# A graph layer on one core: edge tables and reciprocals move from VectorE to ScalarE, and the f32 selection tables read a PSUM ramp

## What is computed

```
xn = layernorm(x)
msg  = xn[src] * edge_weight                    # segment mean per (relation, target), 8 relations
gnn  = einsum(mean of msg, weight) + xn @ root + bias
q, k = elu(xn @ wq + bq) + 1, elu(xn @ wk + bk) + 1 ;  v = xn @ wv + bv       # 8 heads
mix  = ((q @ (k^T v)) / (q . sum(k) + 1e-6)) @ wo + bo
x1 = x + gnn + mix
f  = layernorm(x1)
out = x1 + sum over the 2 best of 6 experts (routing weight * three-layer MLP of f)
```

## Time and profile before

| | |
|---|---|
| time, median of 3 runs | 3027.47 us (3027.4 to 3027.52) |
| the profiled execution | 3028.82 us, its span 3027.3 us |
| PE | 2934.1 us busy (97% of the span) |
| DVE | 2189.2 us (72%) |
| ACT | 1765.7 us (58%) |
| POOL | 1659.3 us (55%) |
| mean granted TensorE clock | 0.988 of full speed |

### The profile page before, as it was taken

One profiled execution on the slowest core, in us unless ns is written; L12 is line 12 of the kernel. 1 busy time (PEld: TensorE's weight loads), 2 busy tenths in 40 slices (PEclk: granted clock), 3 DMA queues, 4 the chain that ended last, 5 costly groups with the idle time before them and its releaser, 6 DMA issues.

```text
span 3027.3 us, 47261 instructions
## 1 busy us (share of the span) xinstructions
PE 2934.1 (97%) x16707; PEld 2567.4 (85%) x16708; DVE 2189.2 (72%) x5317; ACT 1765.7 (58%) x3392; POOL 1659.3 (55%) x1700
## 2 busy tenths in 40 slices
PE   6999999969989999999999999999999999999998
PEld 5888878858778888888888888888888888888887
DVE  4479664125668787778888777788777778878775
ACT  3555555523446665666666566666666566666555
POOL 1000000042257777777777777777777777777740
PEclk9999999989999999999999999999999999999999
DMA  7677677875443444444444444443444444344420
GB/s 258 249 267 272 261 276 269 292 250 174 146 140 107 129 131 132 133 127 129 118 121 133 133 134 129 131 122 118 134 131 131 134 126 129 116 128 131 131 74 11
DMA packets 182224, 473.45 MB, mean 156 GB/s; under 512 B 46934, under 2 KB 105260, under 8 KB 159747
## 3 DMA queue, kind: packets, MB, share of 16 engines
q0 software_dynamic: 80544, 221.54, 25.4%
q1 hardware_dynamic: 99248, 247.02, 22.6%
q10 hardware_dynamic: 2196, 1.86, 0.2%
HBM read 312.80 MB, written 158.29 MB: 156 GB/s over the span
## 4 chain that ended last, share of the span: by engine, by line
PE 68%; DVE 6%; ACT 2%; DVEq 1%; issue 1%; DMA 1%; SPq 0%; ACTq 0%
PE bank L1647 45%; PE acc L1704 8%; PE acc L1710 8%; PE acc L1647 2%; DVE sel L1362 2%; PE bank L1674 1%; PE bank L1810 1%; DVE x L1457 1%; PE bank L1683 1%; PE bank L1693 1%; DVE stats_c L1461 1%; PE bank L1760 1%; DVEq L1459 1%; DVE h_lo L1487 1%; ACT h_hi L1205 1%
## 5 line engine op out<-in xcount | busy, mean ns | idle before, releaser
L1135 POOL DMA_INDIRECT ring<-y_tab,tab x1666 | 1642.6, 986 | 653.4 <-issue 497.5
L1205 ACT ACTIVATE h_hi<-bank,bias_t 128x512 fp32r<-128x512 f32 (+1 forms) x600 | 407.7, 679 | 315.6 <-PE bank L1647 280.1
L1487 DVE TENSOR_TENSOR h_lo<-bank,h_hi 128x512 fp32r<-128x512 f32 (+1 forms) x600 | 382.1, 675 | 228.1 <-ACT bank L1206 226.2
L769 PE MATMUL yb<-wr_hi,xhl 128*128 128x512 f32 x1568 | 509.4, 402 | 14.5 <-ACT yst L350 12.5
L1192 ACT ACTIVATE row_hi<-ring,tab 128x256 fp32r<-128x256 f32 x1091 | 449.6, 497 | 14.4 <-PE acc L1710 13.5
L1379 DVE SCALAR_TENSOR_TENSOR row_lo<-ring,tab,row_hi 128x256 fp32r<-128x256 f32 x1091 | 447.8, 478 | 7.8 <-ACT row_hi L1192 7.8
L350 ACT ACTIVATE yst<-yb 128x512 f32<-128x512 f32 x392 | 229.8, 596 | 273.6 <-PE yb L769 245.5
L1206 ACT ACTIVATE bank<-bank,bias_t 128x512 f32<-128x512 f32 (+1 forms) x600 | 386.3, 644 | 0.0
L769 PEld LDWEIGHTS yb<-wr_hi,xhl 128*128 128x128 f32 x1568 | 298.6, 190 | 88.8 <-ACT yst L350 15.2
L1647 PE MATMUL bank<-ew_hi,h_hi 128*128 128x256 f32 x1176 | 342.7, 291 | 1.5 <-DVE h_lo L1487 1.4
L1647 PE MATMUL bank<-ew_lo,h_hi 128*128 128x256 f32 x1176 | 329.1, 280 | 0.0
(11 more groups left out here) (265 smaller groups left out, 5514.7 us busy)
## 6 DMA issues: line engine op xcount, KB each, us to landing
y_tab<-yst SPq DMA_DIRECT2D x97, 1024.0 KB, 4.1
ring<-y_tab,tab POOLq DMA_INDIRECT x1666, 2.8
xt_tab<-xhl SPq DMA_DIRECT2D x25, 1024.0 KB, 4.6
xk<-xt_tab SPq DMA_DIRECT2D x25, 1024.0 KB, 4.9
xc<-xt_tab SPq DMA_DIRECT2D x25, 1024.0 KB, 5.4
x<-x_tab SPq DMA_DIRECT2D x49, 256.0 KB, 3.2
xs<-in_x SPq DMA_DIRECT2D x24, 512.0 KB, 6.0
x_tab<-xs SPq DMA_DIRECT2D x24, 512.0 KB, 5.0
```

Source lines behind the costliest of these rows:

```text
L769: last = pe.matmul(out_ap, a, b, start=(i == 0), stop=(i == len(parts) - 1))
L1135: pool.indirect_dma_start(out=out_ap, out_offset=None, in_=y_tab[:, :], in_offset=bass.IndirectOffsetOnAxis(ap=idx_ap, axis=0)).then_inc(s ...
L1205: act.activation(dest[:, m, 0:W], b[:, 0:W], ACT.Relu, bias=bias)
L1487: gone(dve.tensor_tensor(lo_[:, m, 0:W], bank[plan[kind, (e, m)][0]][:, 0:W], hi[:, m, 0:W].bitcast(F32), ALU.subtract))
```

## The change

Three edits, all in the second part.

1. `weighted` reads `ramp` (PSUM) in place of `iota_w` (SBUF): every one of the 575 `sel` instructions.
2. `tables` moves to ACT: four activations of 128x17 (identity plus a bias, which is minus the tile's first node, from a new table `neg_t` that POOL writes at the start). In the loop they stand behind `high` of expert 3 in place of the same expert's end on DVE. Tables 0 and 1 are made ahead of all key work on ACT. DVE's `weighted` waits for a new semaphore, `rel_set`.
3. The copy of the reciprocals over features moves to ACT (`by_feature`): one activation of 128x1024, which waits for DVE's reciprocal (`rden_set`). In the loop it stands behind `gate_t` and ahead of `high` of portions 5 and 6.

```diff
+            neg_t = sbuf(pc, "neg_t", [P, TROWS])
...
             @block.gpsimd
+                pool.iota(neg_t[:, :], pattern=[[-NT, TROWS]], base=0, channel_multiplier=0,
+                          allow_small_or_imprecise_dtypes=True).then_inc(neg_set, 1)
...
             @block.scalar
+                def by_feature(i):
+                    act.wait_ge(rden_set, i + 2)
+                    act.activation(rden_c[:, :, :].rearrange("p t (h d) -> p (t h) d", h=HEADS),
+                                   rden[:, :, :].rearrange("p t h -> p (t h)").unsqueeze(2)
+                                   .to_broadcast([P, SUB * HEADS, C // HEADS]), ACT.Copy).then_inc(rden_ready, 1)
+
+                def tables(n):
+                    act.wait_ge(tab_in[n % 2], 16 * SUB * (n // 2 + 1))
+                    for t in range(SUB):
+                        last = act.activation(rel_w[:, n % 2, t, :], tab[:, n % 2, t, :, 1], ACT.Identity,
+                                              bias=neg_t[:, SUB * n + t:SUB * n + t + 1])
+                    last.then_inc(rel_set, 1)
...
                             gone(act.activation(gate_t[:, 0:W], take(i, plan, "gt", 0)[0:GROWS, 0:W], ACT.Copy))
+                        if more and e == 1:
+                            by_feature(i)
                         for p in SPLIT_AT.get(e, ()) if more else ():
                             high(i + 1, p)
+                        if more and e == EXPERTS - 3 and i + 2 < SUPER:
+                            tables(i + 2)
...
+                act.wait_ge(neg_set, 1)
+                tables(0)
+                tables(1)
                 for p in range(PARTS):
...
                     if p == KEYED + 1:
...
+                        by_feature(-1)
...
             @block.vector
                     dve.drain()
-                    dve.reciprocal(rden[:, :, :], rden[:, :, :])
-                    dve.drain()
-                    dve.tensor_copy(rden_c[:, :, :].rearrange("p t (h d) -> p (t h) d", h=HEADS),
-                                    rden[:, :, :].rearrange("p t h -> p (t h)").unsqueeze(2)
-                                    .to_broadcast([P, SUB * HEADS, C // HEADS])).then_inc(rden_ready, 1)
+                    dve.reciprocal(rden[:, :, :], rden[:, :, :]).then_inc(rden_set, 1)
...
-                def tables(n):
-
-                    dve.wait_ge(tab_in[n % 2], 16 * SUB * (n // 2 + 1))
-                    for t in range(SUB):
-                        dve.tensor_scalar(rel_w[:, n % 2, t, :], tab[:, n % 2, t, :, 1], float(n * NS + t * NT), None,
-                                          ALU.subtract)
-                    dve.drain()
-
                 def weighted(n, p):
                     if p >= parts(n):
                         return
+                    dve.wait_ge(rel_set, n + 1)
                     tables_free(dve, n, p)
                     for q, (t, k) in enumerate(tiles_of_portion(p)):
-                        last = dve.tensor_scalar(sel[:, p % BUFS, q, :], iota_w[:, :], rel_w[:, n % 2, t, k:k + 1],
+                        last = dve.tensor_scalar(sel[:, p % BUFS, q, :], ramp[:, 0:NT], rel_w[:, n % 2, t, k:k + 1],
                                                  tab[:, n % 2, t, k, 2:3], ALU.is_equal, ALU.mult)
...
-                        if more and e == EXPERTS - 3:
-                            if i + 2 < SUPER:
-                                tables(i + 2)
```

More of the change, by code:

```diff
@@ L969, in gps_layer @@
             emptied = {"act": sem("act_emptied"), "dve": sem("dve_emptied")}
-            rden_ready, acc_full, x1_done = (sem(n) for n in ("rden_ready", "acc_full", "x1_done"))
+            rden_set, rel_set, rden_ready, acc_full, x1_done = (sem(n) for n in ("rden_set", "rel_set", "rden_ready", "acc_full", "x1_done"))
             var_c, std_c, xn_c, d_ready, ex_ready, gap_ready, g2_ready, gate_ready = (
@@ L987, in gps_layer @@
             rows_in = [sem(f"rows_in{g}") for g in range(SLOTS)]
-            xtab_in, xold_in, xrows_in, xrows_split, xsum_done, xnew_set, xnew_out, base_set, x_tab_done, xsum_free = (
+            xtab_in, xold_in, xrows_in, xrows_split, xsum_done, xnew_set, xnew_out, base_set, neg_set, x_tab_done, xsum_free = (
                 sem(n) for n in ("xtab_in", "xold_in", "xrows_in", "xrows_split", "xsum_done", "xnew_set", "xnew_out",
-                                 "base_set", "x_tab_done", "xsum_free"))
+                                 "base_set", "neg_set", "x_tab_done", "xsum_free"))
             def tiles(plan):
@@ L1573, in _ @@
                 dve.memset(zv[:, :, :, :], 1.0)
-                tables(0)
+                dve.drain()
                 for p in range(PARTS):
@@ L1604, in _ @@
                                           ALU.subtract).then_inc(w_split_c, 1)
-                tables(1)
                 prepare(1, 0)
```

## The result

The changed kernel takes 3063.09 us (median of 4 runs, 3062.6 to 3064.68) against 3027.43 us for the kernel before in the same session: 1.0122 times as long, 95% interval 1.0108 to 1.0137. It is slower by 36 us, and the profiled execution's span grew by 34.5 us, from 3027.3 to 3061.8. Where this time lies can be read from five views of the changed kernel.

The account below looks back on a forecast made before the run. The loop was taken as bound by PE and its turn-end wait for DVE's y; ramp 18.5, copy 15.6 and start 1.5 us sum to 35.6, giving 3063 us, own range 3052 to 3075, 8 in 10 from 3042 to 3086.

Parts of the forecast that it names:

- What bounds the kernel: In the loop PE is the bound; its one recurring wait is for DVE's y at a turn's end, 0.57 us.
- faster: Rival: sel from PSUM begins sooner, shrinking the turn-end wait, worth 13.4 us in all; 3016 without an expert 1 stall; chance 0.06.
- The ramp from PSUM: Twelve sel columns at a turn's end, each 67 ns slower: 0.80 us a turn, +18.5 us (0 to 37).
- The copy over features: ACT's copy in expert 1 delays portion 5's rows 0.97 us against 0.43 slack: 0.65 us x 24, +15.6 us.
- the cold start: In expert 1, PE restarting behind its stall without weights loaded ahead: 0.1 us added, chosen between nothing and 0.39.
- One sign: Expected trace sign in expert 1: DVE's wait for row_hi grows from 0.33 to about 2 us.
- The tables: Four small activations moved to ACT in expert 3, where nobody waits for them: nothing.
- The start: Key features begin 6 us later, covered by PE's 7.76 us wait; portion 11's rows late after key work: +1.5 us.
- The sum: Whole run: 18.5 + 15.6 + 1.5 = 35.6 us more, giving a median of 3063 us.
- one stays away: Rival: the turn-end stall or the expert 1 stall doesn't come, about 3046 us; chance 0.15.
- the two last: Rivals "faster" (3016 without an expert 1 stall; chance 0.06) and no difference, both additions hidden (3027; chance 0.06).
- More than the sum: Rival: turn-end idle of 1.4 us drops PE's clock, up to 3101, or PSUM source at upper bound, 3082; chance 0.13.

Follow-up runs that it names:

- e8: Kernel before with none of the edits, but six sel columns moved behind the additions to y at a turn's end; 3015.56 us, ratio 0.9959.
- e9: Kernel before with tables on ACT and six sel columns moved behind the additions to y at a turn's end; 3019.27 us, ratio 0.9964.
- f2: Kernel before with sel made four ways by portion: PSUM or SBUF source, 64 or 128 columns an instruction; a single execution, 3105.52 us.
- e1: Changed kernel with sel reading the ramp in SBUF again; tables and copy over features stay on ACT; 3044.52 us, ratio 1.0059.
- e3: Kernel before with one edit alone, tables made on ACT; 3026.65 us, ratio 1.0001.
- e2: Changed kernel with the copy over features back on DVE; PSUM ramp and tables on ACT stay; 3046.84 us, ratio 1.0069.
- e4: Kernel before with one edit alone, sel reading the ramp in PSUM; 3047.45 us, ratio 1.0069.
- e5: Changed kernel with ACT's copy over features moved behind the rows of portion 5; 3045.13 us, ratio 1.0047.
- e6: Changed kernel with six of the twelve sel columns at a turn's end moved behind the additions to y; 3029.61 us, ratio 0.9997.
- e7: Changed kernel with the copy moved behind portion 5's rows and six sel columns behind the additions to y; 3022.92 us, ratio 0.9976.
- f1: Changed kernel with ACT's copy over features made three times in a row in expert 1; 3145.49 us, ratio 1.0383.
- f3: Kernel before with tables on ACT, six sel columns behind the additions to y and one extra gather a block; 3038.17 us, ratio 1.0038.

## Why the prediction was right, step by step

- **What bounds the kernel.** Right. Every run in which the wait for `y` at a turn's end grew or shrank moved the time with it. What I hadn't read is the second bound close beneath: POOL waits for PE for only 11.8 us of the loop's 2048, by the same view of waits. My rival "faster" put the turn's end at 13.4 us; with PE's restarts it is 19, of which the loops of e8 and e9 got 7, nearly all of it in their first seven or eight turns; behind these the gathers kept it.
- **The ramp from PSUM.** Forecast 67 ns a column, 0.80 us a turn, 18.5 us. Measured 63 ns (0.319 less 0.256), a run of twelve longer by 0.75 us, PE's wait longer by 1.31 - 0.57 = 0.74 us, 17 us over 23 turns; alone it cost 0.0069, 21 us, with 17 to 25 in the interval. The rate was right and the start unchanged (f2). The Trainium skill ("VectorE: DVE Perf Modes", "Why PSUM operands drop a tier") has the rate so, and f2's 1.05 ns a column agree. The longer start of the Trainium skill's cycle table (the same page, "The TRN2 errata"), which by the prediction's estimate would have made 131 ns a column, isn't in these runs. The five columns ahead of `ft_lo` stayed hidden.
- **The copy over features.** The mechanism was right in each link; the size was a little small. The delay of 0.97 us was 0.94, the slack of 0.43 was 0.40, and `y` came 0.54 us after the moment at which PE would have gone on (its last product's start and one pitch, 1648.76 + 0.23 = 1648.99, against 1649.53). That this is the forecast to the hundredth is luck: two errors of 0.03 us cancel. The term that was mis-sized is the cold start, "a choice" of 0.1 us: PE begins 0.06 us after `y` ends and needs 0.34 us for its first product where the pitch is 0.23, so 0.17 us. 0.71 x 24 = 17 us in place of 15.6; e1 less e3 gives 0.0058, 18 us. The wait that the view of waits shows, 0.43 us, is not the price: it counts from the modelled end of the last product, 0.16 us after the next could have begun. One sign was misread: DVE's wait for `row_hi` was to grow to about 2 us and is 1.29. DVE spends the 0.69 us that it saves on the copy ahead of this place, where it waits for PE's bank before the first additions to `y` (0.89 us in the changed kernel, 0.17 before).
- **The tables.** Next to nothing, as forecast (e3: 1.0001). A turn of e3 takes 87.63 us against 87.58, and one of e2 88.38 against e4's 88.33: 0.05 us, which no ratio here can tell.
- **The start.** The steps happened. ACT's rows and PE's waits in the trace of the changed kernel:

```profile
642.97 0.94 ACT L1197 ACTIVATE rel_w<-tab,neg_t 128x17 f32<-128x17 f32 x4 [8.62 <-DMA tab<-etab]
643.92 1.28 ACT L1271 ACT_TABLE_LOAD   x1
645.22 0.42 ACT L1271 ACTIVATE ek_c<-zv 128x256 f32<-128x256 f32 x1
...
646.45 1.23 PE L1819 MATMUL bank<-zv,kf_c 128*128 128x129 f32 x4 [9.81 <-DVE kf_c L1571]
...
659.15 0.50 PE L1656 MATMUL bank<-wkv_hi,xk 128*128 128x512 f32 x1
...
885.75 0.39 PE L1719 MATMUL acc<-row_hi,hot_r 128*128 128x256 f32 x1 [1.10 <-DVE row_lo L1392]
```

  Key features begin at 645.22 (forecast 645 in place of 638.70), PE waits 9.81 us for them, and yet the third block's products begin at 659.15, where they began at 659.18: the delay went into the cover. At the end of the key work portion 11's rows cost 1.10 us (forecast 1.5). What I had not seen is that the cover has a price of its own, and that it fell. The idle 7.76 us before 659.18 were followed by a low clock; now PE works up to then. The same stretch by windows, before and after:

```profile
659.10:664.00 4.90, 4.82 (x13) 4.00 (x14) 1.02 (x2) 0.72 (x2) 3.68 (x5) 0.50 0.69 239
```
```profile
659.10:664.00 4.90, 4.86 (x26) 4.16 (x26) 2.68 (x6) 2.04 (x6) 3.73 (x4) 1.00 0.85 295
```

  13 products against 26 in the same time. The low clock now stands at the first key products behind the wait of 9.81 us (646.4 to 651.1: 15 products, at 0.50), and its loss fits into the cover too. The move is worth about 2.5 us in a trace: the products of the key work's last portion but one begin at 880.01 in place of 882.75, and behind portion 11 block 0's gates still come 1.2 us earlier (929.84 against 931.01). So the start gained in these two traces what the forecast had it lose. But it is lost in the scatter of the runs: over the traces with the old start (the kernel before, e4, e8, f2) these gates lie between 928.7 and 932.7 us, over those with the whole new one (the changed kernel, e1, e5, e6, e7, f1) between 928.2 and 931.8; and e3, in which the low clock moves too, is not measurably faster.
- **The sum.** 35.6 us forecast, 34.5 in the span. The turns split it more sharply than the ratios do. A turn, from gates to gates, takes 89.10 us in place of 87.58: 1.52 us more, 1.45 forecast. The ramp has 0.75 of it (e4: 88.33), the copy 0.72 (e1 less e3: 88.35 less 87.63), the tables 0.05. So the terms were 17.2 us (forecast 18.5), 17.3 over 24 turns (15.6), 1.2 (nothing) and, for the start, -1.2 (+1.5). Errors of 1.2 to 2.7 us with opposite signs cancelled. That the sum is closer than its parts is luck, and so is a median of 3063.09 for 3063.
- **The rivals.** Both stalls came, so "one stays away" and the two last fell. What "faster" hoped for is there in one respect: no `sel` takes more than 413 ns now, where the slowest took 577, but each begins later after the one before. "More than the sum" was weighed rightly for this kernel, whose 1.31 us at the turn's end leave the clock at 1.00, but its mechanism is real: f1 shows it behind 2.7 us, and f2 and f3 behind less (below).

## What to carry to other kernels

Work moved to an idle engine isn't free where it stands in front of something that a third engine waits for. Look up what is queued behind it on that engine, and measure the slack at the end of the chain, at the engine that bounds, in tenths of a microsecond; a line's place was worth more here than its engine or its source. Before counting on a gain from a shorter wait, look whether the next engine, here the one that issues gathers, has any idle time left in the loop.

## What the runs showed of the hardware

The loop's traces show idle stretches of TensorE of several lengths, and whether the granted clock fell to 0.50 (1.2 GHz) behind them, mostly for 3.4 us:

| idle stretch | where | clock fell |
|---|---|---|
| 1.3 us (at most 1.7) | changed kernel, e2, e4, e5: 23 in each | never |
| 1.7 to 1.8 us | e8 and e9: 4 together | never |
| 1.7 to 1.8 us | f3: 10 | 4 times |
| 2.4 to 2.8 us | f2, at a turn's end: 23 | 14 times |
| 2.7 us | f1, in expert 1: 24 | 17 times |

In f2 a turn in which it fell takes 91.4 us and one in which it didn't 90.0, so a fall costs 1.5 us, as in f1. In f1 and f2 some stretches of one length are spared and others not, with the same products ahead and behind. No run here tells what divides them.
